# Token maxima in quarters of 32 rows, four matmuls in neighbouring row groups, and a token operand spread into per-head columns

## What is computed

```python
enc, ca = ctx[:, :2044, :], ctx[:, 2044:, :]      # 4 tokens ca of 384 channels
query, keyt, valt = x @ Wq, enc @ Wk, enc @ Wv
hs = mha(query, keyt, valt)                       # 8 heads of 80
ca_q1 = einsum('btc,th->bch', ca, Wq_ca)          # 384 rows, of rank 4
ca_q1 = ca_q1[:, indices, :]                      # repeated to 1024 rows
ca_hs1 = mha(ca_q1, x, x)
ca_hs2 = mha(ca_hs1 @ Wq, ca @ Wk_ca, ca @ Wv_ca)
out = (hs + ca_hs2) @ Wout + b_out + x
```

## Time and profile before

| | |
|---|---|
| median of 3 runs | 1228.3 us (1227.75 to 1228.32) |
| the profiled execution, its own time | 1228.01 us |
| its span, from first to last instruction | 1226.2 us |
| granted TensorE clock, mean | 1.000 |
| TensorE busy | 1214.0 us, 99% |
| VectorE, ScalarE, GpSimd busy | 829.0, 679.7, 205.6 us |
| chain that ended last | 99% TensorE |

### The profile page before, as it was taken

The page is one execution under the profiler, slowest core; times in us unless marked ns, Lnnn a source line. Parts: engine busy times, 40 slices in busy tenths (PEclk is TensorE's granted clock), DMA queues, the critical chain, the costliest instruction groups (busy, mean ns, idle before and its releaser), DMA issues.

```text
span 1226.2 us, 14526 instructions
## 1 busy us (share of the span) xinstructions
PE 1214.0 (99%) x5644; PEld 956.8 (78%) x5644; DVE 829.0 (68%) x1168; ACT 679.7 (55%) x773; POOL 205.6 (17%) x114
## 2 busy tenths in 40 slices
PE   7999999999999999999999999999999999999999
PEld 6889888898667677777777777777777777776899
DVE  6439825592244378888878878888888888885552
ACT  6333324222544367677677677677677677778310
POOL 1100000001000011312322222221221221221233
PEclk9999999999999999999999999999999999999999
DMA  8974795793840064154254344344345335332254
GB/s 304 350 284 165 237 344 199 265 315 94 234 115 1 1 194 97 65 151 109 80 137 108 91 126 108 104 119 111 105 112 127 95 103 146 111 91 65 69 211 150
DMA packets 80335, 180.68 MB, mean 147 GB/s; under 512 B 17305, under 2 KB 33945, under 8 KB 76138
## 3 DMA queue, kind: packets, MB, share of 16 engines
q1 hardware_dynamic: 72554, 157.33, 42.5%
q0 software_dynamic: 2816, 11.80, 3.0%
q10 hardware_dynamic: 4896, 10.62, 2.5%
HBM read 116.32 MB, written 63.24 MB: 146 GB/s over the span
## 4 chain that ended last, share of the span: by engine, by line
PE 99%; ACT 0%; DMA 0%; issue 0%; DVE 0%; ACTq 0%
PE at_ps L1232 29%; PE bank L653 20%; PE at_ps L1213 19%; PE at_ps L210 9%; PE acc_t_ps L1009 7%; PE at_ps L1419 6%; PE s_ps L976 2%; PE bank L630 2%; PE bank L600 1%; PE f_ps L949 1%; PE acc_t_ps L987 1%; PE f_ps L210 1%; PE f_ps L928 1%; PE f_ps L938 0%; DMA ctx_f<-in_ctxT 0%; PE at_ps L1422 0%
## 5 line engine op out<-in xcount | busy, mean ns | idle before, releaser
L218 DVE TENSOR_REDUCE mpart<-at_ps 128x1 f32<-128x512 f32 x480 | 326.7, 687 | 109.7 <-PE at_ps L210 108.1
L1154 ACT ACTIVATE prob_hi<-at_ps 128x1024 fp32r<-128x1024 f32 (+1 forms) x256 | 263.2, 1028 | 194.4 <-PE at_ps L1213 194.4
L1232 PE MATMUL at_ps<-prob_hi,v 128*81 128x512 f32 (+1 forms) x1024 | 318.9, 396 | 0.2 <-issue 0.2
L1091 DVE TENSOR_TENSOR prob_lo<-probs,prob_hi 128x1024 fp32r<-128x1024 f32 (+1 forms) x211 | 271.1, 1285 | 23.4 <-ACT probs L1159 23.4
L1159 ACT ACTIVATE probs<-at_ps 128x1024 f32<-128x1024 f32 (+1 forms) x256 | 261.1, 1020 | 0.0
L1232 PEld LDWEIGHTS at_ps<-prob_hi,v 128*81 128x81 f32 (+1 forms) x1024 | 153.8, 151 | 59.5 <-issue 6.1
L1091 POOL TENSOR_TENSOR prob_lo<-probs,prob_hi 128x1024 fp32r<-128x1024 f32 x45 | 108.1, 2402 | 519.7 <-ACT probs L1159 519.7
L210 PE MATMUL at_ps<-a 128*128 128x512 f32 x480 | 194.2, 405 | 0.0
L210 PEld LDWEIGHTS at_ps<-a 128*128 128x128 f32 x480 | 153.6, 320 | 32.0 <-DVE mpart L218 1.3
L1213 PE MATMUL at_ps<-a 128*128 128x512 f32 (+1 forms) x512 | 161.5, 396 | 1.2 <-ACT probs L1159 0.6
L1213 PE MATMUL at_ps<-b 113*128 113x512 f32 (+1 forms) x512 | 160.6, 394 | 0.0
(11 more groups left out here) (144 smaller groups left out, 1452.8 us busy)
## 6 DMA issues: line engine op xcount, KB each, us to landing
v_hi_d<-v_t SPq DMA_DIRECT2D x16, 648.0 KB, 6.4
v_lo_d<-v_t SPq DMA_DIRECT2D x16, 648.0 KB, 8.5
v<-v_hi_d SPq DMA_DIRECT2D x16, 648.0 KB, 4.8
v<-v_lo_d SPq DMA_DIRECT2D x16, 648.0 KB, 5.9
k_hi_d<-out_hi SPq DMA_DIRECT2D x40, 256.0 KB, 4.8
k_lo_d<-out_lo SPq DMA_DIRECT2D x40, 256.0 KB, 5.4
a<-k_hi_d SPq DMA_DIRECT2D x16, 640.0 KB, 7.3
b<-k_hi_d SPq DMA_DIRECT2D x16, 640.0 KB, 10.9
```

The source lines that it names most:

```text
L218: dve.tensor_reduce(self.mpart[:, g % 2, qt, c:c + 1], mx_ps[k % 2][:, 0:w], AX, ALU.max).then_inc(self.mx_done, 1)
L1091: eng.tensor_tensor(pl[n % PB][0:r, :], prob[n % PF][0:r, :], ph[n % PB][0:r, :].bitcast(F32), ALU.subtract).then_inc(sem, 1)
L1154: act.activation(ph[n % PB][0:r, :], s_ps[n % 2][0:r, :], ACT.Exp, scale=SCALE).then_inc(ph_done, 1)
L1232: mm = pe.matmul(o_ps[:, u * CH:(u + 1) * CH], a[0:r, t, :], y[n % PB][0:r, u * CH:(u + 1) * CH], start=t == 0 and m == 0, stop=t == KT - ...
```

## The change

The rows of `u` and of the tokens' operand get a new layout. Head h has its 12 rows (three products by four tokens) and a 13th for the shift from row `32 * (h % 4) + 16 * (h // 4)` on, so that each quarter of 32 rows holds two heads, h and h + 4. The operand `ca` has for each batch and each value of `h // 4` a block of 384 columns, in which a quarter holds the one head's rows and zeros in the other's. An m job now takes one quarter, 32 rows, and four m jobs with the four quarters follow each other, into four banks; they are instructions for tile positions 0, 32, 64 and 96 of the array with 32 rows each, where the matmuls of before were all for the whole array. There are still 48 in each batch, in 12 groups of four. `GROUPS_AT` puts the groups behind the five q jobs of chunk 1, behind three k and three v jobs of chunk 2 and behind one k job of chunk 3.

`ca` for both batches is loaded once (`ca_raw`, 128 by 1536) and split once, in batch 0. Since rows of different products need other signs and parts, high and low are formed with a scale and a bias for each row from a small array `marks`. For `tokens`, `spread_tokens` copies a head's 384 columns and multiplies them by 1 in the head's quarter and 0 in the others, 8 times for each batch on ScalarE: for batch 1 at the v jobs of chunk 0 in batch 1, for batch 0 at heads 2 and 3 of `tokens`. The score matmul takes all 128 rows. The second and third load of `caBD` and their splits are gone, as is the row of ones that POOL set. All eight shifts of batch 1 are issued by POOL; those of batch 0 stand later in SP's queue.

```diff
-CA_PARTS = 4
+GROUPS_AT = {("q", 1): (0, 1, 2, 3, 4), ("k", 2): (0, 2, 4), ("v", 2): (1, 4, 7), ("k", 3): (1,)}
+def token_row(h):
+    return 32 * (h % 4) + 16 * (h // 4)
+def quarter(h):
+    return slice(32 * (h % 4), 32 * (h % 4 + 1))
...
-        jobs, maxima = [], [("m", 0, (hc, u)) for hc in range(NH * KC) for u in range(2)]
+        jobs = []
+        maxima = [(top, kc, u) for u in range(2) for top in range(NH // 4) for kc in range(KC)]
+
+        def with_maxima(some, c):
+
+            for i, job in enumerate(some):
+                jobs.append(job)
+                if i in GROUPS_AT.get((job[0], c), ()):
+                    top, kc, u = maxima.pop(0)
+                    jobs.extend(("m", u, (4 * top + r, kc, u)) for r in range(4))
...
-                    if c == 1:
+                    if b == 0 and c == 1:
                         pool.wait_ge(w_lo, 3)
...
+                        pool.dma_start(ca_raw[:].rearrange("p (b n) -> p b n", b=B),
+                                       d["ca_rows"].rearrange("b k n -> k b n")).then_inc(ca_in, 16)
+            pool.wait_ge(ca1_done, NH)
             pool.wait_ge(top_done, 2 * B)
-            shift_tokens(pool, kept, ca, B - 1, range(1, NH, 2))
+            shift_tokens(pool, kept, ca1, B - 1)
...
+            def split_ca():
+                act.wait_ge(ca_in, 16)
+                act.activation(ca[:], ca_raw[:], ACT.Identity, scale=marks[:, 3:4]).then_inc(ca_hi, 1)
...
+                    if b == 1 and kind == "v" and c == 0:
+                        spread_ca(m[1] * CH // P + m[0])
...
-                        act.activation(dst, banks[n % 8][0:K3, :], ACT.Copy).then_inc(hi_done, 1)
...
+                        act.activation(dst, banks[n % 8][:], ACT.Identity, bias=marks[:, 2:3], scale=marks[:, 0:1]
+                                       ).then_inc(hi_done, 1)
...
+                dve.wait_ge(ca_hi, 1)
+                dve.scalar_tensor_tensor(out=ca[:], in0=ca_raw[:], scalar=marks[:, 4:5],
+                                         in1=ca[:].bitcast(F32), op0=ALU.mult, op1=ALU.add).then_inc(ca_lo, 1)
...
+                        dve.scalar_tensor_tensor(out=dst, in0=bank[:], scalar=marks[:, 1:2], in1=dst.bitcast(F32),
+                                                 op0=ALU.mult, op1=ALU.add).then_inc(done, 1)
...
-                        hc, u = m
-                        if (hc, u) == (0, 0):
-                            pe.wait_ge(ca_lo, b + 2)
-                            pe.wait_ge(done, b * NJ + last["u", NQ - 1] + 1 + 8)
-                        at = hc // KC * CD + hc % KC
-                        pe.matmul(bank[:], ca[0:K3, at:at + (P - 1) * KC + 1:KC],
-                                  u_all[0:K3, bass.ds(b * SQ + u * CH, CH)], start=True, stop=True
+                        h, kc, u = m
+                        if (h, kc) == (0, 0):
+                            pe.wait_ge(ca_lo, 1)
+                            pe.wait_ge(done, b * NJ + last["u", u] + 1 + 8)
+                        at = (b * 2 + h // 4) * CD + kc
+                        pe.matmul(bank[:], ca[quarter(h), at:at + (P - 1) * KC + 1:KC],
+                                  u_all[quarter(h), bass.ds(b * SQ + u * CH, CH)], start=True, stop=True
...
+def spread_tokens(act, kept, to, b, h):
+
+    at = (b * 2 + h // 4) * CD
+    return act.activation(to[:, h * CD:(h + 1) * CD], kept["ca"][:, at:at + CD].bitcast(F32), ACT.Copy,
+                          scale=kept["marks"][:, 5 + h % 4:6 + h % 4])
...
-            sp.wait_ge(ca_lo, CA_PARTS)
+            sp.wait_ge(kept["ca_lo"], 1)
...
+            sp.wait_ge(ca0_done, NH)
+            shift_tokens(sp, kept, ca[0], 0)
             at.shift(sp, 0)
...
-                    if n == 3:
-                        act.wait_ge(kept["ca0_in"], 16)
-                        act.activation(ca[0][0:K3, ca_part(j)], ca_f[0:K3, ca_part(j)], ACT.Copy).then_inc(ca_hi, 1)
+                    if n in (2, 3):
+                        spread_tokens(act, kept, ca[0], 0, (n - 2) * pairs + j).then_inc(ca0_done, 1)
...
-                                   kept["u"][0:K3 + 1, b * SQ + st * P:b * SQ + (st + 1) * P],
-                                   ca[b][0:K3 + 1, h * CD:(h + 1) * CD], start=True, stop=True)
+                                   kept["u"][:, b * SQ + st * P:b * SQ + (st + 1) * P],
+                                   ca[b][:, h * CD:(h + 1) * CD], start=True, stop=True)
```

More of the change, by code:

```diff
@@ L304, in project @@
         stages = [("wk", flat[:, 0:n_k]), ("wv", flat[:, n_k:2 * n_k]),
-                  ("wqca", flat[:, 2 * n_k:2 * n_k + MC * K3]), ("wq", ca_f[:])]
+                  ("wqca", flat[:, 2 * n_k:2 * n_k + MC * P]), ("wq", ca_f[:])]
         stages = [(n, v.rearrange("p (m n) -> p m n", m=w[n][0].shape[1])) for n, v in stages]
-        jobs, maxima = [], [("m", 0, (hc, u)) for hc in range(NH * KC) for u in range(2)]
-        for c in range(NS):
[L311 to L316, removed]
+        jobs = []
[6 more added lines that the diff above has]
+                    jobs.extend(("m", u, (4 * top + r, kc, u)) for r in range(4))
+        for c in range(NS):
+            with_maxima([("k", c, m) for m in range(MC)], c)
+            with_maxima([("v", c, (t, u)) for u in range(2) for t in range(4)], c)
             if c < NQ:
-                jobs += [("q", c, m) for m in range(MC)] + [("u", c, 0)]
+                with_maxima([("q", c, m) for m in range(MC)], c)
+                jobs.append(("u", c, 0))
         assert not maxima
@@ L324, in project @@
         last = {(kind, c): n for n, (kind, c, _) in enumerate(jobs)}
-        last_m = last["m", 0]
+        last_m = last["m", 1]
         def read_ctx(c):
@@ L668, in project, with shift_tokens @@
         return Stage(sync, gpsimd, scalar, vector, tensor), written, evicted
-def shift_tokens(eng, kept, ca, b, some):
-    for h in some:
-        row = ca[K3:K3 + 1, h * CD:(h + 1) * CD].rearrange("o (p c) -> o p c", c=KC)
+def spread_tokens(act, kept, to, b, h):
+    at = (b * 2 + h // 4) * CD
+    return act.activation(to[:, h * CD:(h + 1) * CD], kept["ca"][:, at:at + CD].bitcast(F32), ACT.Copy,
+                          scale=kept["marks"][:, 5 + h % 4:6 + h % 4])
+def shift_tokens(eng, kept, ca, b):
+    for h in range(NH):
+        r = token_row(h) + 3 * NT
+        row = ca[r:r + 1, h * CD:(h + 1) * CD].rearrange("o (p c) -> o p c", c=KC)
         eng.dma_start(row.bitcast(F32), kept["ntop"][:, b, h * KC:(h + 1) * KC].bitcast(F32)
@@ L989, in token_scores @@
                 mm.then_inc(t_full, 1)
-            pe.wait_ge(kept["u_ones"], 1)
             total = len(heads) * pairs
@@ L1539, in layouts @@
     ca = ctx[:, SK:, :]
-    wqca = np.zeros((NH, D, 3, NH, NT), Wq_ca.dtype)
-    ca_bd = np.zeros((B, 3, NH, NT, NH, CD), ctx.dtype)
+    wqca = np.zeros((NH, D, P), Wq_ca.dtype)
+    ca_rows = np.zeros((B, P, 2, CD), ctx.dtype)
+    marks = np.zeros((P, 9), np.float32)
+    marks[:, 0] = marks[:, 3] = 1
     for h in range(NH):
-        for r in range(3):
-            wqca[h, :, r, h, :] = Wq_ca[:, h * D:(h + 1) * D].T
-            ca_bd[:, r, h, :, h, :] = ca
+        r = token_row(h)
+        for i in range(3):
+            wqca[h, :, r + i * NT:r + (i + 1) * NT] = Wq_ca[:, h * D:(h + 1) * D].T
+            ca_rows[:, r + i * NT:r + (i + 1) * NT, h // 4, :] = ca
+        low_u, low_ca = slice(r + 2 * NT, r + 3 * NT), slice(r + NT, r + 2 * NT)
+        marks[low_u, 0], marks[low_u, 1], marks[r + 3 * NT, 2] = -1, 1, 1
+        marks[low_ca, 3], marks[low_ca, 4] = -1, 1
+        marks[quarter(h), 5 + h % 4] = 1
     mask = np.zeros((NH, D, NH), np.float32)
```

89 lines of the change are left out of this document (34 added, 55 removed).

## The result

The changed kernel takes 1220.1 us (median of 6 runs, 1219.5 to 1220.9) against 1228.3 (6 runs, 1227.75 to 1228.8): a ratio of 0.9934 [0.9921, 0.9947], 8.2 us or 0.66% faster. The forecast was 1215.3 in a range of 1211.0 to 1229.5, with a chance of 0.68 for faster. The sign and the range hold; of the 13.0 us that were reckoned, 8.2 came. The granted clock is 1.0 of full speed, 2.4 GHz, in both profiled executions.

What follows compares the result with a forecast made beforehand. TensorE, busy 99% of the span, was taken as the bound. -23.0 (m jobs out) + 9.6 (groups) + 0.4 (wait) = -13.0 us, from 1228.3 to 1215.3 us, in a range of 1211.0 to 1229.5.

Steps and rivals of the forecast that it cites:

- The m jobs out, -23.0: TensorE, chunks 2 and 3: the old m jobs cost 11.5 us a batch, so removing them saves 23.0 us.
- Side by side: TensorE: a group's four matmuls run at once, g 0.25 to 0.57; the forecast case, chance 0.55.
- The three rivals that need them one after another: TensorE groups: loads serial, 1225.1, chance 0.15; no overlap, 1228.3 to 1229.7, 0.15; array empties, 1247.5 at 1.74, slower 0.12.
- g: What one group of four m jobs adds to TensorE's line: 0.40 us used, 24 groups 9.6 us.
- The upper bound of 0.57: Group cost with one matmul tail showing at the entry and one at the exit: 24 groups 13.7 us, time 1219.4.
- the slower rival: TensorE's array runs empty between whole and quarter layout, 0.99 to 1.74 us a group; chance 0.12 for clearly slower.
- The rule of a 3.07-fold gain: Skill's figure for four packed 32-row matmuls on TensorE: g would be 0.31, groups 7.3 us, time 1213.0.
- The other rule: Skill's statement that changing TensorE's tiling mode drains the engine, weighed under the array running empty, chance 0.12.
- The wait for `ca`, +0.4: Batch 0, first group behind the first q job of chunk 1: TensorE waits 0.4 us once for the split.
- VectorE and the banks, nothing: Chunk 2: VectorE falls 0.3 us behind, then gains 1.4; eight banks cover it, so no cost.
- Copies and shifts: ScalarE's spread copies fit beside v evictions and in the token stage; POOL's and SP's shifts land in time: no cost.
- the cover of 22 us: Token stage: batch 0's shifts on SP's queue land by 331 us, some 22 us ahead of that batch's first scores.

Runs made afterwards that it cites:

- e3: The changed kernel with each m job a matmul over all 128 rows, at the same places and into the same banks: 1226.8 us.
- e4: The changed kernel with two of the four matmuls in each group, and their maxima, left out: 1220.4 us.
- e8: e4 with two pairs at each of half as many places (12 for 24): 1214.3 us.
- e2: The changed kernel with an unused tile of 128 bytes in each partition ahead of the context's buffers: 1222.0 us.
- e6: The changed kernel with the split of `ca` eight v jobs earlier: 1219.9 us.
- e10: The changed kernel with 16 places of six m jobs instead of 24 of four, and m-job weights that lie in a row: 1217.0 us.
- e11: e10 with 12 places of eight m jobs: 1232.9 us.
- e1: The kernel before, with an unused tile of 128 bytes in each partition ahead of the context's buffers: 1227.2 us.

## Why the prediction was right, and where it was off

**The m jobs out, -23.0.** Held: e3, with four full matmuls at each place, adds 0.94 to 0.96 a group, 22.6 to 23.0 for the 24, as much as was taken out. It lies 1.5 us under the kernel before, by the medians and by the stretch, and the other two effects, the pace (-2.0) and the wait (+0.5), make -1.5.

**Side by side.** Right as a mechanism: four matmuls and four weight loads in one row each, and e4's half costs as much. The three rivals that need them one after another (0.81 a group, 0.94 to 1.0, 1.74) fall.

**What a group costs: the step that failed.** The forecast was g = 0.25 + 0.16 = 0.40, "one time in a group something shows that is hidden in a plain row". Measured are 0.70 to 0.73, 24 x 0.72 = 17.3 us for 9.6, so 7.7 us of the gain are missing. By the prediction's own sign ("wrong if g is not 0.25 to 0.57") this step is wrong, though the time lies in its range. The upper bound of 0.57 had one tail at the entry and one at the exit, but took the weight loads as hidden. What happens is the working of the slower rival, in which the array runs empty and loads in the open; that one was summed to 0.99 with the four together, with a tail of 0.16, load and run of the group of 0.25 + 0.39, and a load of 0.19, where the rows above have 0.09, 0.51 and 0.10. The argument against it, that 96 rows beside 128 rows cost nothing now, was about rows of one layout and said nothing on the change to 32. For a g of 0.72 the sum would have been -23.0 + 17.3 + 0.4 = -5.3 and 1223.0.

The rule of a 3.07-fold gain for four packed matmuls ("TensorE: Matmul & The Clock Gate", part 3, of the Trainium skill) doesn't show at a group between full matmuls: 0.96 by e3 to 0.73 is 1.3-fold. The other rule weighed there does: that a change of the tiling mode drains the engine ("TensorEngine Tiling (Array Packing)", tiling modes, of the Trainium skill) agrees with the 0.35 and 0.25 us of idle time of the weight loads around the group, and with e8, where the second set in one layout costs 0.23.

**The pace of the k and u jobs, in no term.** 0.233 to 0.227 us for 315 matmuls of k jobs, about 1.7 us, given back by where the buffers came to lie; e2 loses as much again, 1.7 by the stretch and 1.9 by the medians. The u jobs went from 0.231 to 0.227, some 0.3 us for 60 matmuls; their weights grew from 96 to 128 columns, and no run tests the cause. Together 2.0. It hides part of the error in g, and that is luck: without it the result would have been about 1222.

**The wait for `ca`, +0.4.** 0.47, once, at 74.16. The split took 71.11 to 74.54, 3.4 us for 3.27.

**The balance.** -23.0 + 17.3 + 0.5 - 2.0 = -7.2, and the stretch is 7.5 us shorter. The first score matmul of the token stage starts at 274.26, before it was 281.92: 7.7 us sooner, and not 13. The spans differ by 8.1, the medians by 8.2; the half us behind the projection was not traced to a cause (from the first score matmul to the end it is 944.3 us before, 943.8 in the changed kernel and 944.1 in e6, which has the same token stage).

**VectorE and the banks, nothing.** Right: no wait of TensorE for VectorE in the projection, and e4 without half of the maxima is no faster. How near it was e10 and e11 tell.

**Copies and shifts.** A spread copy is 0.61, not "more like half" of 0.83; it stayed beside v jobs and in the token stage as reckoned. POOL's shifts are issued from 261.8 on, 4.8 us behind the start of the last group (257.0) where 1.0 was reckoned, and the last is there by 265.6 + 4.5 = 270.1, 4.2 ahead of the token stage instead of 7. For SP's of batch 0 the price was far off: "eight issues (0.6 each, 5 us) and the landing (4.2)" are in the trace 17.3 us of issues and 10.9 to 23.8 to landing. Timeline of SP's queue and of TensorE in the changed kernel, and the landing of these eight:

```profile
316.33 17.34 SPq L707 DMA_DIRECT2D ca<-ntop  x8
...
344.90 0.59 PE L997 MATMUL s_ps<-ca,u 128*128 128x384 f32 x2
...
DMA to landing us min/median/max: 10.9/21.0/23.8
```

The first shift, issued at 316.3 with 23.8 to landing, is there by 340.1, the last (330.4 and 10.9) by 341.3; the first scores of batch 0 start at 344.9. Of the cover of 22 us about 4 are left. The shifts stand behind the loads of `a` and `v`, which keep the DMA engines over 90% busy until about 335 us (a share of 0.97 or more in every five us from 310 on, 0.36 from 335 to 340). Nothing waited, so the term of nothing held, but its working did not.

## What to carry to other kernels

Small matmuls on a quarter of the array do run side by side, but between full matmuls a place with them costs a change of layout there and back: here 0.72 us for the first set of up to four and 0.23 for the next two, against 0.96 for four full ones. So gather as many sets at one place as the banks allow (here six matmuls; the banks of the jobs just ahead are still being evicted), and give them weights that lie in a row, since nothing hides their loads. When adding up such an edit, ask of each operation not only what it takes but whether its weight load still lies over the matmul ahead; and where layouts of memory shift, look at the pace of the untouched work too.

## What the runs showed of the hardware

- A plain row of 128 x 512 matmuls went at 0.227 or 0.233 us each by where the operands lay: with 128 bytes more ahead of the context's buffers the k jobs change from one to the other, in both directions (e1, e2). The chosen distances are 0 and 128 modulo 256; others were not tried, and near the m jobs of the old kernel the effect is weaker.
- The weight load on 32 rows with a step of three elements took 246 ns, with none 181; on 128 rows with the step 252 (e3).
- Eight DMA issues of 1.5 KB each took 0.5 us apiece on POOL's queue, landing in 3.5 to 4.5, though the DMA engines were as busy then (a share of 1.03 from 260 to 266 us); and 17.3 us together, landing in up to 23.8, on SP's queue behind large loads.
